# Causal masking of the diagonal blocks moved from two-pass score matmuls to Pool, in a one-core pre-norm transformer layer

## The chip, the cores and the metric

The kernel runs on one core of one Trainium2 chip. The metric is the device time of one launch in microseconds. A core has a matrix engine (PE: matmuls, with weight loads shown apart as PEld), a vector engine (DVE), a scalar engine (ACT), a general engine (Pool) and SyncE (SP), whose queue issues the DMAs here. Each runs its own instructions in order and they meet by semaphores.

## The reference

One attention block with ALiBi bias and causal mask, then a gated feed-forward block with ternary weights, both with a layer norm ahead and a residual. T = 2048 tokens, D = 256, 16 heads of 16, hidden 704.

```
s = q @ k.T / 4 + slope[h] * (key - 2047)          # per head; the bias hangs on the key alone
s = where(key <= query, s, lowest float)
attn = softmax(s);  x = x + (attn @ v) @ Wo + bo
x = x + bitlinear(sigmoid(bitlinear(n, w1)) * bitlinear(n, w2), w3)    # n = layernorm(x)
```

## The kernel before

Queries are taken in four chunks of 512 (c = 0 to 3), heads in four groups of four; chunk times group makes 16 units. A unit of chunk c walks over 4(c+1) key blocks of 128: that is a **step**, 160 in all. In one step each of the four heads gets one transposed score tile, keys on the partitions and up to 512 queries along the row. The last four steps of a unit are its **diagonal steps** (64 in all; in chunk 0 every step is one): there the tile starts at the diagonal block (`q0`), so its width is 512, 384, 256 and 128.

A score matmul (L928) contracts two stacks of 128 rows, `kst` and `qst`: 64 rows of query and key in split high and low parts, two rows of ALiBi, padding, and two rows that subtract the row maximum. On a diagonal step a second matmul (L931, bf16, an identity times the 128x128 triangle `maskb`) adds -3e38 to the future keys of the diagonal block. ACT then takes exp from PSUM into a slot of `probs` (L775; seven slots, three PSUM banks), and PE multiplies the slot with the values (L941, `weighted`; ones beside the values give the denominators).

PE's order is written out: in step s come scores of head 0, head 1, a **side group** (projections, feed-forward matmuls of a neighbouring chunk), head 2, then `weighted(s-1)` for the four heads, then head 3. After each head's scores stand **max turns** of the next unit (L908: scores the other way round, into three banks `pM`), which DVE reduces to row maxima (L1078, L1081 with mask). The turns are dealt out over the steps by a planned room of DVE. A unit's maxima then go to `qst` by DMA (L448) before its first score.

Pool's work per step is one instruction group in order: `split_lo` (L671, gates the store of q and k parts, and ACT's next projection), `split_hidden` (L650, L652, gates the down projection), setting up of stack rows (`key_rows` L658 and `query_rows` L663, L664), `add_bo` (L641), `norm_ctx` (L603) and `power` for the layer norm (L632, DVE's `normalise` L999 waits for it). The head of the program builds `ident`, `mask`, `maskb` on Pool (L613 to L625), then loads the first stacks through SP (`load_k` L427, L429; `load_q` L442), whose landing the first turn waits for.

Of the kernel before, what the change touches and what calls it, by code (L numbers as in the profile page):

```python
# [16 lines left out]
def preln_layer(nc, x, Wq, bq, Wk, bk, Wv, bv, Wo, bo, w1, w2, w3, alibi, out):  # L17
# [24 lines left out]
    R_END = P  # L42
    R_MAX = R_END - 2
    KSLOTS, QSLOTS, PSLOTS = 7, 4, 7
# [9 lines left out]
    phase0 = [first_step[c * NHG] for c in range(NCH)] + [NS]  # L54
    steps = [(u, j) for u in range(NU) for j in range(n_steps[u])]


# [39 lines left out]

    POST_AT = [None, 10, 22, 41]
    late = [("up", NCH - 2, 1, FT - 2), ("up", NCH - 2, 1, FT - 1), ("down", NCH - 2, 1)]
# [101 lines left out]
    with es:  # L201
# [42 lines left out]
        ones = flat[:, 6 * CH:6 * CH + P]  # L244
        w_abs = flat[:, 0:FT * D]
        x2T = sb("x2T", [P, 2, KT, HALF], F32R)
        hT = sb("hT", [P, 2, FT, HALF], F32R)
        mask = sb("mask", [P, CH], BF16)
        maskb = sb("maskb", [P, P], BF16)
        ident = sb("ident", [P, P])  # L250
# [51 lines left out]
        const_ok = sem("const_ok")  # L302
        pad_ok = sem("pad_ok")
        rows_ok = sem("rows_ok")
        k_rows = sem("k_rows")
# [23 lines left out]
        scores_ready = sem("scores_ready")  # L329
        probs_ready = sem("probs_ready")  # L330
        pv_done = sem("pv_done")
        ctx_saved = sem("ctx_saved")
# [13 lines left out]
        def diag(u, j):  # L346

            return max(0, j - TPC * units[u][0]) * P

        def is_diag(u, j):  # L350
            return j >= TPC * units[u][0]

# [25 lines left out]
        def _(sp):  # L378
# [37 lines left out]
            def load_k(n):  # L416
                v, i = pieces[n]
                parts_there("k", i, units[v][1])
                if n >= KSLOTS:

                    pu, pi = pieces[n - KSLOTS]
                    sp.wait_ge(scores_ready, G * (first_step[pu] + TPC * pi + TPC))
                if n < KSLOTS:
                    sp.wait_ge(k_rows, n + 1)
                hg = units[v][1]
                src = part_rows(1, i, hg).rearrange("d (p a) h n -> (d p) a (h n)", a=1)
                sp.dma_start(kst[0:R_ALIBI, n % KSLOTS, :, :].bitcast(F32),  # L427
                             src.to_broadcast([2 * HD, 2, G * CH])).then_inc(k_in[n % KSLOTS], 16)
                sp.dma_start(kst[R_ALIBI:R_ALIBI + 2, n % KSLOTS, :, :].bitcast(F32),  # L429
                             alibi_parts[:, hg * G:(hg + 1) * G, i * CH:(i + 1) * CH])\  # L430
                    .then_inc(k_in[n % KSLOTS], 16)

            def load_q(v):
# [6 lines left out]
                for a in range(2):  # L440
                    src = part_rows(0, c, hg)[:, a:a + 1, :, :].rearrange("d a h n -> d a (h n)")
                    sp.dma_start(qst[a:R_ALIBI:2, v % QSLOTS, :, :].bitcast(F32),  # L442
                                 src.to_broadcast([HD, 2, G * CH])).then_inc(q_in[v % QSLOTS], 16)

            def load_m(v):
# [144 lines left out]
        def _(pool):  # L590
# [18 lines left out]
            for i in range(2):  # L609
# [10 lines left out]
                                         fill=NEG, base=0, pattern=[[-1, P]], channel_multiplier=1))  # L620
            link(nc.gpsimd.memset(maskb[:, :], 0.0))

            link(nc.gpsimd.affine_select(out=maskb[:, :], in_=maskb[:, :], compare_op=ALU.is_ge, fill=NEG,
                                         base=0, pattern=[[1, P]], channel_multiplier=-1))
            nc.gpsimd.memset(ones, 1.0).then_inc(const_ok, 1)  # L625

            pool.wait_ge(const_ok, 1)


# [31 lines left out]
            def query_rows(n):  # L661
# [3 lines left out]
                pool.wait_ge(q_rows, n + 1)  # L665

            def split_lo(g):
                i = split_no[g]
# [6 lines left out]
            power(1)  # L675
            query_rows(0)
            split_lo(("k", 0, 0))
            power(2)
# [10 lines left out]
            for s, (u, j) in enumerate(steps):  # L689
                c = units[u][0]  # L690
                ph = s - phase0[c]
                g = side[s]
                if g and g[0] in "kq":
                    split_lo(g)
# [4 lines left out]
                if ph == 2 and c >= 1:  # L699
                    add_bo(c - 1)  # L700
                if c >= 1 and ph == POST_AT[c] - 2:
                    norm_ctx(c - 1)
# [113 lines left out]
        def _(pe):  # L816
# [80 lines left out]
            def max_turn(u, k):  # L897
                i, h, t = turn_of(u, k)
                c = units[u][0]
                if k == 0:  # L900
                    pe.wait_ge(q_in[u % QSLOTS], Q_DMAS * 16 * (u // QSLOTS + 1))
                n = piece0[u] + i
                if h == 0 and t == 0:
                    pe.wait_ge(k_in[n % KSLOTS], K_DMAS * 16 * (n // KSLOTS + 1))
                x = ("turn", u, k)
# [12 lines left out]
            def scores(s, h):  # L918
# [4 lines left out]
                if j == 0 and h == 0:  # L923
# [3 lines left out]
                b = j % TPC * P  # L927
                ins = pe.matmul(pS[:, n % SBANKS, q0:CH], kst[0:R_END, sl, h, b:b + P],  # L928
                                qst[0:R_END, u % QSLOTS, h, q0:CH], start=True, stop=not is_diag(u, j))
                if is_diag(u, j):  # L930
                    ins = pe.matmul(pS[:, n % SBANKS, q0:q0 + P], identb[:, :], maskb[:, :], start=False, stop=True)  # L931
                ins.then_inc(scores_ready, 1)

            def weighted(s):
# [4 lines left out]
                for h in range(G):  # L939
                    pe.wait_ge(probs_ready, G * s + h + 1)  # L940
                    pe.matmul(pO[32 * h:32 * h + VW, q0:CH], vals[:, j, units[u][1] * G + h, :],  # L941
# [282 lines left out]
```

## Time and profile before

| | us |
|---|---|
| median of 3 runs | 697.68 (695.25 to 704.3) |
| profiled execution | 701.53, its span 698.6 |
| granted TensorE clock, mean | 0.972 |

The span is the time between the first and the last instruction; the execution's time is 2.9 us more. Busy shares of PE are of modelled ends; matmuls are pipelined, so distances between starts tell what a matmul costs.

### The profile page before, as it was taken

Reading aid. Unit: us, or ns where it says so; the run is one execution under the profiler, and the core shown is the slowest. Engines: PE = TensorE matmul, PEld = TensorE weight load, DVE = VectorE, ACT = ScalarE, POOL = GpSimd, SP = SyncE. Lnnn points to the kernel's source line nnn. Section 1 sums busy time; section 2 is a strip of 40 time slices with the busy share of each in tenths; the row PEclk is TensorE's granted clock in tenths of the full one; section 3 lists DMA queues with packets and bytes.
Section 4 is the critical chain, followed back from the end, with each engine's and each line's share of the span. In section 5 each row is a group of like instructions: output and inputs, shape, how many; then the busy total and the mean of one; then the engine's idle time right before and its main releaser. Section 6 shows DMA issues by size and latency. Waiting matters only on the chain.

```text
span 698.6 us, 10974 instructions
## 1 busy us (share of the span) xinstructions
PE 644.3 (92%) x3710; PEld 373.3 (53%) x3710; DVE 469.8 (67%) x1189; ACT 373.5 (53%) x770; POOL 119.8 (17%) x148
## 2 busy tenths in 40 slices
PE   1788898999999989999999999999999999899997
PEld 1444554546465555455555565555454555456486
DVE  4377858767876866668787778778778787511076
ACT  2424454664564435656655545466576675486621
POOL 5485000041021111320001212003100000031200
PEclk9969988999999999999999999999999999999999
DMA  8665564465131312543221131136131120011000
GB/s 247 179 161 152 138 142 108 95 198 140 32 77 33 92 32 69 177 124 79 62 72 39 32 91 33 47 90 164 44 76 33 47 64 0 2 41 40 1 16 30
DMA packets 26635, 57.64 MB, mean 83 GB/s; under 512 B 4756, under 2 KB 14484, under 8 KB 22996
## 3 DMA queue, kind: packets, MB, share of 16 engines
q1 hardware_dynamic: 26580, 56.95, 31.5%
q8 instruction: 29, 0.48, 0.3%
q14 instruction: 26, 0.21, 0.1%
HBM read 41.87 MB, written 14.80 MB: 81 GB/s over the span
## 4 chain that ended last, share of the span: by engine, by line
PE 79%; DVE 11%; issue 3%; DMA 3%; ACT 2%; SPq 1%; POOL 1%; POOLq 0%; DVEq 0%; ACTq 0%
PE pS L928 20%; PE pO L941 19%; PE pM L908 18%; PE pW L883 5%; DVE pm L1078 3%; PE pW L829 3%; PE pW L892 3%; DVE pM L1081 2%; PE pS L931 2%; PE pW L869 2%; PE pW L835 2%; PE pS L892 1%; DMA qst<-mT 1%; PE pS L829 1%; PE pS L883 1%
## 5 line engine op out<-in xcount | busy, mean ns | idle before, releaser
L775 ACT ACTIVATE probs<-pS 128x512 f32<-128x512 f32 (+3 forms) x640 | 312.9, 536 | 259.9 <-PE pS L931 127.8
L1078 DVE TENSOR_REDUCE pm<-pM 128x1 f32<-128x512 f32 x384 | 243.9, 683 | 70.5 <-PE pM L908 69.8
L908 PE MATMUL pM<-kst,qst 126*128 126x512 f32 (+3 forms) x640 | 244.0, 408 | 17.6 <-DVE pm L1081 7.7
L928 PE MATMUL pS<-qst,kst 128*128 128x512 f32 (+3 forms) x640 | 255.4, 416 | 4.0 <-DMA qst<-mT 3.3
L928 PEld LDWEIGHTS pS<-qst,kst 128*128 128x128 f32 x640 | 121.7, 193 | 138.2 <-ACT probs L775 112.1
L1081 DVE CUSTOM_DVE_ANT_0 pM<-pM,mask 128x128 f32<-128x128 f32 (+3 forms) x256 | 120.7, 514 | 72.0 <-PE pM L908 71.1
L941 PE MATMUL pO<-probs,vals 128*17 128x512 f32 (+3 forms) x1280 | 151.1, 543 | 0.0
L908 PEld LDWEIGHTS pM<-kst,qst 126*128 126x128 f32 x640 | 124.4, 199 | 49.7 <-DVE pm L1081 16.9
L931 PE MATMUL pS<-maskb,identb 128*128 128x128 bf16 x256 | 59.5, 234 | 0.0
L632 POOL TENSOR_TENSOR rstd<-ve,mhalf 128x4 f32<-128x4 f32 (+1 forms) x9 | 8.5, 945 | 240.5 <-DVE ve L994 240.4
L941 PEld LDWEIGHTS pO<-probs,vals 128*17 128x17 f32 x1280 | 21.4, 95 | 42.4 <-issue 31.8
L931 PEld LDWEIGHTS pS<-maskb,identb 128*128 128x128 bf16 x256 | 25.1, 98 | 31.0 <-issue 23.3
L650 POOL CAST hT<-work 128x256 fp32r<-128x256 f32 (+1 forms) x34 | 13.5, 396 | 160.1 <-DVE work L1046 135.3
L1081 DVE DVE_READ_ACCUMULATOR2_ANT pm<- 128x1 f32 x256 | 36.2, 141 | 0.0
L671 POOL TENSOR_TENSOR qk_hl<-qk_f,qk_hl 128x512 fp32r<-128x512 f32 x16 | 20.4, 1275 | 78.4 <-ACT qk_hl L732 78.2
L1046 DVE SCALAR_TENSOR_TENSOR work<-work,pW 128x256 f32<-128x256 f32 (+1 forms) x38 | 15.7, 414 | 26.6 <-ACT work L765 24.1
L883 PE MATMUL pW<-x2T,w1T 128*128 128x256 f32 (+1 forms) x144 | 24.9, 295 | 4.1 <-DVE x2T L1039 2.4
L652 POOL TENSOR_TENSOR hT<-work,hT 128x256 fp32r<-128x256 f32 (+1 forms) x34 | 25.0, 735 | 2.7
L883 PEld LDWEIGHTS pW<-x2T,w1T 128*128 128x128 f32 (+1 forms) x144 | 19.9, 182 | 8.7 <-DVE x2T L1039 2.8
L883 PE MATMUL pW<-x2T,w2T 128*128 128x256 f32 (+1 forms) x144 | 23.4, 285 | 0.0
L883 PEld LDWEIGHTS pW<-x2T,w2T 128*128 128x128 f32 (+1 forms) x144 | 19.8, 184 | 0.0
L892 PE MATMUL pW<-w3T,hT 128*128 128x256 f32 (+1 forms) x120 | 18.1, 295 | 0.3 <-DVE x2T L1039 0.3
(145 smaller groups left out, 425.1 us busy)
## 6 DMA issues: line engine op xcount, KB each, us to landing
kst<-parts SPq DMA_DIRECT2D x40, 512.0 KB
parts<-qk_hl SPq DMA_DIRECT2D x32, 256.0 KB, 3.0
qst<-parts SPq DMA_DIRECT2D x32, 256.0 KB, 4.3
ctx_dram<-ctx_raw SPq DMA_DIRECT2D x15, 256.0 KB, 4.7
xin<-in_L_attn_x SPq DMA_DIRECT2D x5, 512.0 KB, 5.4
out<-work SPq DMA_DIRECT2D x8, 256.0 KB, 2.2
work<-ctx_dram SPq DMA_DIRECT2D x7, 256.0 KB
work<-rden_dram SPq DMA_DIRECT2D x7, 256.0 KB
```

The source lines that it names most:

```text
L652: nc.gpsimd.tensor_tensor(hT_of(g)[0:rows, 1, m, :], hid[0:rows, i % 2, :], hT_of(g)[0:rows, 0, m, :].bitcast(F32), ALU.subtract).then_inc ...
L671: nc.gpsimd.tensor_tensor(lo.bitcast(F32R), qk_f[:, :], hi, ALU.subtract).then_inc(split_ok, 1)
L775: nc.scalar.activation(probs[:, n % PSLOTS, q0:CH], pS[:, n % SBANKS, q0:CH], ACT.Exp)\
L829: ins = pe.matmul(w, (wk_s if kind == "k" else wq_s)[:, k, g[2] * P:(g[2] + 1) * P], xnT[:, k, :], start=k == 0, stop=k == KT - 1)
L883: ins = pe.matmul(w[0:r, i * HALF:(i + 1) * HALF], wT[:, k, m * P:m * P + r], x2T_of(g)[:, part, k, :], start=k == 0 and part == 0, stop=k ...
L892: ins = pe.matmul(w[:, i * D:(i + 1) * D], hT_of(g)[0:r, part, f, i * P:(i + 1) * P], w3T[0:r, f, :], start=f == 0 and part == 0, stop=f = ...
L908: pe.matmul(max_bank(x)[:, 0:N], qst[0:R_MAX, u % QSLOTS, h, t * P:(t + 1) * P], kst[0:R_MAX, n % KSLOTS, h, 0:N], start=True, stop=True). ...
L928: ins = pe.matmul(pS[:, n % SBANKS, q0:CH], kst[0:R_END, sl, h, b:b + P], qst[0:R_END, u % QSLOTS, h, q0:CH], start=True, stop=not is_diag ...
L931: ins = pe.matmul(pS[:, n % SBANKS, q0:q0 + P], identb[:, :], maskb[:, :], start=False, stop=True)
L941: pe.matmul(pO[32 * h:32 * h + VW, q0:CH], vals[:, j, units[u][1] * G + h, :], probs[:, (G * s + h) % PSLOTS, q0:CH], start=j == 0, stop=j ...
L1078: nc.vector.tensor_reduce(dst, bank, AX.X, ALU.max).then_inc(max_free, 1)
L1081: nc.vector.tensor_tensor_reduce(out=sc, in0=sc, in1=mask[:, CH - (t + 1) * P:CH], scale=1.0, scalar=NEG, op0=ALU.add, op1=ALU.max, accum_ ...
```

## The change

The future keys of the diagonal block are no longer pushed down in PSUM. ACT takes exp of the raw tile, and Pool then sets the future keys of the 128x128 diagonal block in the slot to zero with one select (`clear_future`), 256 in all, ahead of its other work of the step; PE's `weighted` waits for Pool (`causal_ok`) on diagonal steps. The 256 matmuls of L931 and `maskb` are gone. Four rows of each stack (124 to 127) are given to half blocks: row b is 1 for the upper half of the keys of block b, and -2^100 for the lower half of the queries of block b, so that the quadrant furthest in the future is exp(-huge) = 0. The two rows of the maximum move to 122 and 123; off the diagonal the matmul uses 124 rows. Pool builds these rows once (`cut_rows`), SP copies them into the 7 + 4 stack slots (`load_cut`), and the slots' semaphores count 16 more. `norm_ctx` in chunk 2 comes one step earlier (at step 19 of the chunk in place of 20; 8 and 39 stay in chunks 1 and 3).

```diff
+    R_CUT = R_END - TPC
+    R_MAX = R_CUT - 2
+    FAR = -2.0 ** 100
-    POST_AT = [None, 10, 22, 41]
+    POST_AT, NORM_AT = [None, 10, 22, 41], [None, 8, 19, 39]
@@ SP
             def load_k(n):
...
+                if n < KSLOTS:
+                    load_cut(kst, cut_k, n, k_in, K_DMAS)
+            def load_cut(stack, cut, n, landed, dmas):
+                if n == 0:
+                    sp.wait_ge(cut_ok, 1)
+                    src = cut
+                else:
+                    sp.wait_ge(landed[0], (dmas + 1) * 16)
+                    src = stack[R_CUT:R_END, 0, 0, :].bitcast(F32)
+                sp.dma_start(stack[R_CUT:R_END, n, :, :].bitcast(F32),
+                             src.rearrange("p (a n) -> p a n", a=1).to_broadcast([TPC, G, CH]))\
+                    .then_inc(landed[n], 16)
@@ Pool
-            link(nc.gpsimd.memset(maskb[:, :], 0.0))
-            link(nc.gpsimd.affine_select(out=maskb[:, :], in_=maskb[:, :], ...))
+            def cut_rows():
+                link(nc.gpsimd.memset(cut_k, 0.0))
+                link(nc.gpsimd.memset(cut_q, 0.0))
...
+                link(nc.gpsimd.affine_select(out=upper, in_=upper, compare_op=ALU.not_equal, fill=1.0, ...))
+                nc.gpsimd.affine_select(out=lower, in_=lower, ..., fill=FAR, ...).then_inc(cut_ok, 1)
+            def clear_future(s, h):
+                u, j = steps[s]
+                n, q0 = G * s + h, diag(u, j)
+                pool.wait_ge(probs_ready, n + 1)
+                block = probs[:, n % PSLOTS, q0:q0 + P]
+                nc.gpsimd.affine_select(out=block, in_=block, compare_op=ALU.is_ge, fill=0.0, base=0,
+                                        pattern=[[1, P]], channel_multiplier=-1).then_inc(causal_ok, 1)
...
             query_rows(0)
+            cut_rows()
             split_lo(("k", 0, 0))
...
+                if on_diag[s]:
+                    for h in range(G):
+                        clear_future(s, h)
+                    pool.wait_ge(causal_ok, G * diag_before[s + 1])
                 if g and g[0] in "kq":
                     split_lo(g)
...
-                if c >= 1 and ph == POST_AT[c] - 2:
+                if ph == NORM_AT[c]:
                     norm_ctx(c - 1)
@@ PE
-                ins = pe.matmul(pS[:, n % SBANKS, q0:CH], kst[0:R_END, sl, h, b:b + P],
-                                qst[0:R_END, u % QSLOTS, h, q0:CH], start=True, stop=not is_diag(u, j))
-                if is_diag(u, j):
-                    ins = pe.matmul(pS[:, n % SBANKS, q0:q0 + P], identb[:, :], maskb[:, :], start=False, stop=True)
-                ins.then_inc(scores_ready, 1)
+                rows = R_END if on_diag[s] else R_CUT
+                pe.matmul(pS[:, n % SBANKS, q0:CH], kst[0:rows, sl, h, b:b + P], qst[0:rows, u % QSLOTS, h, q0:CH], start=True, stop=True).then_inc(scores_ready, 1)
             def weighted(s):
...
-                    pe.wait_ge(probs_ready, G * s + h + 1)
+                    if on_diag[s]:
+                        pe.wait_ge(causal_ok, G * diag_before[s] + h + 1)
+                    else:
+                        pe.wait_ge(probs_ready, G * s + h + 1)
```

## Rows read from the trace of the kernel before

**Rows 1.** The page: busy us (share of the span) and instructions, part 1
```profile
PE 644.3 (92%) x3710; PEld 373.3 (53%) x3710; DVE 469.8 (67%) x1189; ACT 373.5 (53%) x770; POOL 119.8 (17%) x148
```
**Rows 2.** The page: lines of the chain that ended last, part 4
```profile
PE pS L928 20%; PE pO L941 19%; PE pM L908 18%; PE pW L883 5%; DVE pm L1078 3%; PE pW L829 3%; PE pW L892 3%; DVE pM L1081 2%; PE pS L931 2%; PE pW L869 2%; PE pW L835 2%; PE pS L892 1%; DMA qst<-mT 1%; PE pS L829 1%; PE pS L883 1%
```
**Rows 3.** Windows: chunk 0, chunk 1 with the start of 2; stretch, busy (instructions), clock, DMA
```profile
49.90:128.50 78.60, 67.77 (x395) 38.78 (x394) 57.43 (x182) 36.03 (x80) 11.45 (x8) 0.89 0.52 126
128.50:333.00 204.50, 196.78 (x1126) 113.82 (x1127) 144.41 (x363) 112.41 (x233) 36.86 (x46) 0.99 0.38 98
```
**Rows 4.** The same view, a unit's four diagonal steps in chunk 3 (columns PE, PEld, DVE, ACT, POOL)
```profile
497.20:508.60 11.40, 11.40 (x80) 5.66 (x79) 8.96 (x23) 6.81 (x16) 0.00 (x0) 1.00 0.21 50
```
**Rows 5.** Timeline of PE, off the diagonal: scores and turns, 512 wide (start, duration)
```profile
514.17 0.40 PE L928 MATMUL pS<-qst,kst 128*128 128x512 f32 x1
514.40 0.40 PE L908 MATMUL pM<-kst,qst 126*128 126x512 f32 x1
514.64 0.39 PE L928 MATMUL pS<-qst,kst 128*128 128x512 f32 x1
```
**Rows 6.** Timeline of PE, on the diagonal: scores 384 wide, mask matmul, turn
```profile
501.42 0.33 PE L928 MATMUL pS<-qst,kst 128*128 128x384 f32 x1
501.60 0.23 PE L931 MATMUL pS<-maskb,identb 128*128 128x128 bf16 x1
501.64 0.48 PE L908 MATMUL pM<-kst,qst 126*128 126x512 f32 x1
501.95 0.33 PE L928 MATMUL pS<-qst,kst 128*128 128x384 f32 x1
```
**Rows 7.** Timeline, start of Pool's work: select, next instruction; memset 512 wide
```profile
2.11 0.29 POOL L614 TENSOR_SCALAR_AFFINE_SELECT ident<-ident 128x128 f32<-128x128 f32 x1 [0.24 <-POOL ident L613]
2.46 0.29 POOL L616 CAST identb<-ident 128x128 bf16<-128x128 f32 x1
2.81 0.53 POOL L617 MEMSET mask<- 128x512 bf16 x1
```
**Rows 8.** Timeline: ACT ends, Pool starts; Pool ends, ACT starts
```profile
21.15 0.68 ACT L732 ACTIVATE qk_hl<-pS,bias_k 128x512 fp32r<-128x512 f32 x1
21.98 1.26 POOL L671 TENSOR_TENSOR qk_hl<-qk_f,qk_hl 128x512 fp32r<-128x512 f32 x1 [9.64 <-ACT qk_hl L732]
23.33 0.69 ACT L731 ACTIVATE qk_f<-pS,bias_q 128x512 f32<-128x512 f32 x1 [1.50 <-POOL qk_hl L671]
```
**Rows 9.** Timeline, a unit's third diagonal step: exps (head 3 first), weighted matmuls
```profile
506.80 0.55 ACT L775 ACTIVATE probs<-pS 128x256 f32<-128x256 f32 x2 [1.06 <-PE pS L931]
507.86 0.63 PE L941 MATMUL pO<-probs,vals 128*17 128x256 f32 x8
```
**Rows 10.** Timeline of Pool and PE at the end of chunk 1
```profile
264.14 1.01 POOL L632 TENSOR_TENSOR rstd<-ve,mhalf 128x4 f32<-128x4 f32 x1
265.16 0.84 PE L941 MATMUL pO<-probs,vals 128*17 128x384 f32 x8
```
**Rows 11.** Timeline of SP and PE in the head: first loads, first turn
```profile
27.89 0.49 SPq L429 DMA_DIRECT2D kst<-alibi_parts  x1
29.70 1.19 SPq L442 DMA_DIRECT2D qst<-parts  x2
35.07 1.12 PE L908 MATMUL pM<-kst,qst 126*128 126x128 f32 x3 [3.31 <-DMA qst<-parts]
```
**Rows 12.** Timeline of DVE: normalise beside Pool's memset, and alone
```profile
8.63 4.50 DVE L999 TENSOR_SCALAR xin<-xin,mv,rstd 128x256 f32<-128x256 f32 x4 [1.22 <-POOL rstd L632]
125.84 1.36 DVE L999 TENSOR_SCALAR xin<-xin,mv,rstd 128x256 f32<-128x256 f32 x4
```
**Rows 13.** Timeline: Pool's long work beside a reduction of DVE
```profile
490.10 2.67 POOL L603 TENSOR_TENSOR work<-work 128x512 f32<-128x512 f32 x2 [6.95 <-DMA work<-rden_dram]
490.78 0.69 DVE L1078 TENSOR_REDUCE pm<-pM 128x1 f32<-128x512 f32 x1 [0.58 <-PE pM L908]
```
**Rows 14.** Timeline of ACT: the last exp of the last step
```profile
661.26 0.28 ACT L775 ACTIVATE probs<-pS 128x128 f32<-128x128 f32 x1 [0.61 <-PE pS L931]
```

More of the change, by code:

```diff
@@ L42, in preln_layer @@
     R_END = P
-    R_MAX = R_END - 2
+    R_CUT = R_END - TPC
+    R_MAX = R_CUT - 2
+    FAR = -2.0 ** 100
     KSLOTS, QSLOTS, PSLOTS = 7, 4, 7
@@ L55, in preln_layer @@
     steps = [(u, j) for u in range(NU) for j in range(n_steps[u])]
+    on_diag = [j >= TPC * units[u][0] for u, j in steps]
+    diag_before = [sum(on_diag[:s]) for s in range(NS + 1)]
     piece0 = [sum(units[v][0] + 1 for v in range(u)) for u in range(NU + 1)]
@@ L245, in preln_layer @@
         w_abs = flat[:, 0:FT * D]
+        cut_k, cut_q = ctx_raw[0:TPC, :], probs[0:TPC, 3, :]
         x2T = sb("x2T", [P, 2, KT, HALF], F32R)
@@ L248, in preln_layer @@
         mask = sb("mask", [P, CH], BF16)
-        maskb = sb("maskb", [P, P], BF16)
         ident = sb("ident", [P, P])
@@ L303, in preln_layer @@
         pad_ok = sem("pad_ok")
+        cut_ok = sem("cut_ok")
         rows_ok = sem("rows_ok")
@@ L330, in preln_layer @@
         probs_ready = sem("probs_ready")
+        causal_ok = sem("causal_ok")
         pv_done = sem("pv_done")
@@ L348, in diag @@
             return max(0, j - TPC * units[u][0]) * P
-        def is_diag(u, j):
-            return j >= TPC * units[u][0]
         def max_bank(x):
@@ L443, in load_q @@
                                  src.to_broadcast([HD, 2, G * CH])).then_inc(q_in[v % QSLOTS], 16)
+                if v < QSLOTS:
+                    load_cut(qst, cut_q, v, q_in, Q_DMAS)
             def load_m(v):
@@ L620, in _ @@
                                          fill=NEG, base=0, pattern=[[-1, P]], channel_multiplier=1))
-            link(nc.gpsimd.memset(maskb[:, :], 0.0))
-            link(nc.gpsimd.affine_select(out=maskb[:, :], in_=maskb[:, :], compare_op=ALU.is_ge, fill=NEG,
-                                         base=0, pattern=[[1, P]], channel_multiplier=-1))
             nc.gpsimd.memset(ones, 1.0).then_inc(const_ok, 1)
             pool.wait_ge(const_ok, 1)
+            def cut_rows():
+                link(nc.gpsimd.memset(cut_k, 0.0))
+                link(nc.gpsimd.memset(cut_q, 0.0))
+                upper = cut_k.rearrange("p (b e n) -> p b e n", b=TPC, e=2)[:, :, 1, :]
+                lower = cut_q.rearrange("p (b e n) -> p b e n", b=TPC, e=2)[:, :, 0, :]
+                link(nc.gpsimd.affine_select(out=upper, in_=upper, compare_op=ALU.not_equal, fill=1.0, base=0,
+                                             pattern=[[-1, TPC], [0, P // 2]], channel_multiplier=1))
+                nc.gpsimd.affine_select(out=lower, in_=lower, compare_op=ALU.not_equal, fill=FAR, base=0,
+                                        pattern=[[-1, TPC], [0, P // 2]], channel_multiplier=1).then_inc(cut_ok, 1)
+                pool.wait_ge(cut_ok, 1)
             def power(n, t0=0, t1=TPC):
@@ L900, in max_turn @@
                 if k == 0:
-                    pe.wait_ge(q_in[u % QSLOTS], Q_DMAS * 16 * (u // QSLOTS + 1))
+                    pe.wait_ge(q_in[u % QSLOTS], 16 + Q_DMAS * 16 * (u // QSLOTS + 1))
                 n = piece0[u] + i
                 if h == 0 and t == 0:
-                    pe.wait_ge(k_in[n % KSLOTS], K_DMAS * 16 * (n // KSLOTS + 1))
+                    pe.wait_ge(k_in[n % KSLOTS], 16 + K_DMAS * 16 * (n // KSLOTS + 1))
                 x = ("turn", u, k)
```

## The prediction, made before the changed kernel was run

> **What bounds the kernel now.** I read the page's busy shares first, then the lines of the chain, then the windows of each chunk, and at last the timelines of single steps. PE is busy 92% of the span, DVE 67%, Pool 17% [rows 1]. The chain runs over PE's scores, weighted matmuls and max turns for 57% of the span, and DVE's reductions for 5% [rows 2]. By chunk: in chunk 0 PE is busy 67.8 of 78.6 us and DVE 57.4, at a granted clock of 0.89, so both take turns to hold up the other; from chunk 1 into chunk 2 PE is busy 196.8 of 204.5 us and DVE 144.4, 71% [rows 3]. In the four diagonal steps of a unit of chunk 3 PE has no idle time at all in 11.40 us, and DVE has 8.96 us of work [rows 4]. So PE's order of matmuls sets the time, and DVE stands 21% behind it just where the change works.
>
> **The mask matmul's price.** Its busy time of 0.23 us [rows 6] is no price, since matmuls overlap. Distances between starts are: off the diagonal a score tile and a turn, both 512 wide, repeat every 0.47 us (514.17 to 514.64), of which the score tile takes 0.23 and the turn 0.24 [rows 5]. On the diagonal a 384-wide score tile, the mask and a turn repeat every 0.53 us [rows 6]. Without the mask the tile would take 384/512 of 0.23, that is 0.17, and the turn 0.24: 0.41. The mask costs 0.12 us. In the start times only 0.04 of that stands between the mask and the turn (501.60 to 501.64); the rest is that the turn's successor starts 0.31 after it, in place of 0.24. Lower bound: 0.04, the mask's own distance. Upper bound: the whole 0.23 of its busy time, as if nothing overlapped. I take 0.12, because it compares whole repeats.
>
> A rule of the Trainium skill differs: "TensorE: Matmul & The Clock Gate", section Back-to-back issue gap, puts a stream of weight load and matmul pairs at N = 128 at about 81 ns each. By that estimate 256 of them are 20.7 us, of which the shares taken below leave 15.8, 11.9 net: 686 us. The trace's repeats give 0.12 a piece, half as much again.
>
> In chunks 1 to 3 there are 48 diagonal steps with 192 masks: 192 x 0.12 = 23.0 us of PE. A unit's four diagonal steps lose 16 x 0.12 = 1.9 us, 11.40 to 9.5, with DVE's 8.96 unchanged: DVE goes to 94%. It may run only three banks apart from PE, so some of PE's gain turns into waits for turns; I take 85%, 19.6 us. The bound for this is DVE's own 8.96: no more than 2.4 us a unit, 29 us for 12 units. In chunk 0, 64 x 0.12 = 7.7 us, and since DVE holds PE for part of it I take half, 3.8 us. Gain: 23.4 us.
>
> **What Pool adds.** 256 selects of 128x128 f32. The same form took 0.29 us, and the next instruction started 0.35 us after it [rows 7]. Four a step are 1.4 us, 90 us in all; Pool goes from 17% to some 30%. That is under the mean diagonal step of chunk 3, 11.40 / 4 = 2.85 now and 2.4 after [rows 4]. DVE's reductions read PSUM and take no harm: one took 0.69 us in the middle of a Pool instruction of 2.67 [rows 13].
>
> What counts is the delay from the last exp of a step (head 3) to `weighted`. ACT's end to Pool's start took 0.15 (21.83 to 21.98), Pool's end to the next engine 0.09 (23.24 to 23.33) [rows 8]: 0.15 + 0.29 + 0.09 = 0.53 us. PE leaves room for it, since `weighted(s-1)` stands behind three score tiles of the next step. The room is tightest in a unit's third diagonal step, whose tiles are narrow while the next ones are narrower still: two exps take 0.55 us from 506.80, so head 3's ends near 507.15, and the weighted matmuls start at 507.86: 0.7 us [rows 9]. The mask of the score tile in between goes out of that room, 0.12, and a little more as PE comes sooner: some 0.5 is left, level with the 0.53. I take 0.1 us of stall in each of 12 units, 1.2 us; the wider steps have more room. Queued behind that wait on PE are head 3's scores and the next step; ACT waits for these.
>
> **The in-order queue of Pool.** In a diagonal step the clears stand ahead of `split_lo`, `split_hidden` and `power`, which then wait for the last exp of the step. These ran a step later than PE's start of it anyway, because DVE or ACT were later. The other way round, a clear waits behind the previous step's work. This bites once: at the end of chunk 1 `power` ends at 265.15 and the weighted matmuls of the next diagonal step started at 265.16 [rows 10]; four clears after it are 4 x 0.35 = 1.4 us, of which I take 1.2 on the path. The other long Pool works (`add_bo`, `norm_ctx`) have steps off the diagonal between them and the next clear; uncovered they would cost their own 1.3 us each. Moving `norm_ctx` costs nothing for that reason. `key_rows` of slots 4 to 6 slide some microseconds later in chunk 0, ahead of loads seven steps on.
>
> **Head and tail.** `cut_rows` adds two memsets and two selects 512 wide; a 512-wide memset took 0.53 [rows 7], so some 2.5 us, less 0.6 for `maskb`. Pool was idle for 9.64 us before its first split [rows 8]: hidden; uncovered it is 1.9 us. SP issues 11 small DMAs of some 0.49 us each, the price of the alibi rows' issue [rows 11]. The one for keys falls in the gap from 28.38 to 29.70. The one for queries is issued behind the two of L442 that end at 30.89, whose landing releases the first turn at 35.07 [rows 11]. It lands 0 to 1 us after them; I take 0.5 us. The nine later ones wait only for slot 0's landing, long past. The rows are taken from padding, and 124 or 128 rows make the same columns, so I put that at nothing. At the end, the last exp ended at 661.54 and ACT's copy of the context waits for the weighted matmuls behind it [rows 14]: there the 0.53 less the direct hand-off of 0.1 is bare, 0.4 us. The last unit has no turns, so its room is smaller: 3 steps x 0.2 = 0.6.
>
> **The two-port rule.** DVE's `normalise` took 4.50 us beside a Pool memset and 1.36 alone [rows 12]. Three of them fall in diagonal steps. If each meets Pool's 1.4 us of clears, 3 x 1.4 = 4 us at most; DVE is not the bound there and I count nothing, but keep 4 for the range. This is what the Trainium skill says in "GPSIMD Engine Reference", section 1, Specifications: Pool shares its SBUF interfaces with DVE instructions in a two-port mode. The trace agrees; by the rule at its full price the forecast would be 682 us.
>
> **Sum.** Gain 23.4; costs 1.2 + 1.2 + 0.5 + 0.4 + 0.6 = 3.9; net 19.5. The profiled execution took 701.5 us (span 698.6 and 2.9 around it), 3.8 above the median of 697.7. 701.5 - 19.5 = 682.0 in its own time, and 697.7 - 19.5 = 678.2, so 678 us, against the median.
>
> **Rivals.**
>
> *PE's gain turns into waits for DVE, or the mask was cheaper than a repeat shows.* For it: 94% for DVE after the change, three banks, and the 0.04 between mask and turn; 2% of the span is L931's share of the chain, 14 us [rows 2]. Against it: whole repeats. If half the 23.4 stays, 11.7 - 3.9 = 8 us net, 690 us; with the chain's 14 us, 10 net, 688. Time: 689 us.
>
> *Pool becomes the bound of the diagonal steps (slower).* Place: the four clears of each of the 48 diagonal steps of chunks 1 to 3, on Pool one behind another, with `weighted` waiting for the last. After the change such a step has 2.4 us of PE (9.5 / 4). With t from one select's start to the next, Pool needs 4t: it fills the step at t = 0.6; it eats the net 19.5 us at 4t = 2.4 + 19.5 / 48, t = 0.70; it makes the kernel slower by 2% at 48 x (4t - 2.4) = 19.5 + 14, t = 0.77. At t = 0.85: 48 x 1.0 = 48 us, 697.7 - 19.5 + 48 = 726 us. For it: Pool's spans are rough, the one row of this form is of the idle head, and Pool's 512-wide work takes 1.26 us [rows 8]. Against it: the row gives t = 0.35 [rows 7], less than half of what is needed.
>
> *The mask was dearer.* At 0.18 a mask and DVE in step, 29 us in chunks 1 to 3 and 6 in chunk 0, less 4: 31 net, 667 us.
>
> **How the numbers follow.** Chances: forecast 0.55 (its own range 671 to 683), DVE or cheap mask 0.27, Pool late 0.10, dearer mask 0.08. Faster by over 2%, which is about what a measurement of this kernel can tell from no change (below 683.7): 0.55 + 0.08 = 0.63. Within 2%: 0.27. Slower: 0.10. The range goes from 668 (the dearer mask) to 692 (the lower bound of 0.04 a mask still gives 256 x 0.04 = 10, less the costs of 4, that is 691.5).
>
> **What the changed profile would show.** No L931; score tiles 384 wide and turns repeating every 0.41 to 0.43 us; a unit's four diagonal steps in chunk 3 at 9.5 to 10 us in place of 11.40, with DVE busy over 90% of them; Pool at about 30% with selects of 0.29 us; PE's waits for Pool at `weighted` under 5 us in all. I would be wrong if the four diagonal steps stay above 10.7 us, if selects take over 0.5 us, or if waits for max turns grow by over 8 us.

## The result and the profile after

The changed kernel takes 690.71 us (median of 4 runs, 686.79 to 692.86) beside 697.68 before: a ratio of 0.988, 95% interval 0.983 to 0.993. By that ratio it is faster by 1.2%, and by the two medians by 7.0 us, where 19.5 us (2.8%) were forecast. The time lies inside the forecast's outer range (668 to 692) and outside the forecast's own (671 to 683). Single executions of one kernel lie up to 9 us apart, and the profiled one of the changed kernel, 686.79 with a span of 684.9, was the fastest of its four, so its span of 13.7 us less overstates the gain. Steps inside the profiles repeat far better, and the accounts below are made in them.

One thing has to be kept apart there: the clock that TensorE was granted, which has two levels, 1.2 and 2.4 GHz (0.5 and 1.00 in the profile). Unit 14's steps off the diagonal took 44.36 us at a mean of 0.97 in the kernel before, and 42.97 at 1.00 in the changed kernel: those 1.4 us are no effect of the change, for kernel e2 below, which has the change as well, took 44.15 at 0.97. In the kernel before it fell to 0.50 at 597.8 us, after PE had been busy for 6.20 of 7.80 us; what made it fall was not found. Where two kernels are compared below at unequal clock, the text says so.

The page of the changed kernel, part 1, and three of its groups (line, engine, operation, count, busy us, mean ns, idle before and releaser):

```profile
PE 619.7 (90%) x3454; PEld 360.1 (53%) x3454; DVE 473.1 (69%) x1189; ACT 367.4 (54%) x770; POOL 197.4 (29%) x406
...
L981 PE MATMUL pO<-probs,vals 128*17 128x512 f32 (+3 forms) x1280 | 152.1, 540 | 1.2 <-POOL probs L699 1.2
L699 POOL TENSOR_SCALAR_AFFINE_SELECT probs<-probs 128x128 f32<-128x128 f32 x256 | 74.8, 305 | 245.2 <-ACT probs L815 240.0
L981 PEld LDWEIGHTS pO<-probs,vals 128*17 128x17 f32 x1280 | 22.1, 95 | 46.4 <-issue 35.4 <-POOL probs L699 6.0 <-ACT probs L815 2.2
```

256 matmuls are gone, and Pool stands at 29%, as forecast; a select takes 0.305 us on average in the dense phase, so the price of [rows 7] held. PE's weight loads waited for Pool at the weighted matmuls for 6.0 us in all; what that cost is measured in e2.

The same windows view as [rows 4], the four diagonal steps of unit 12 in the changed kernel:

```profile
487.50:498.00 10.50, 10.40 (x64) 5.24 (x63) 8.85 (x23) 6.21 (x16) 4.21 (x15) 1.00 0.22 53
```

11.40 us became 10.50 with DVE's work unchanged; 9.5 was forecast. PE's timeline in the second of these steps answers to [rows 6]:

```profile
491.02 0.34 PE L969 MATMUL pS<-qst,kst 128*128 128x384 f32 x1
491.20 0.40 PE L948 MATMUL pM<-kst,qst 122*128 122x512 f32 x1
491.43 0.34 PE L969 MATMUL pS<-qst,kst 128*128 128x384 f32 x1
491.61 0.40 PE L948 MATMUL pM<-kst,qst 122*128 122x512 f32 x1
```

The repeat is 0.41 us where it was 0.53: just what was forecast. So the measured repeat was right, and yet half of the time expected from it is missing in this unit. PE's weight loads in the same stretch show some of it, waits that were not there before (in brackets: idle before, releaser):

```profile
488.43 0.19 PEld L948 LDWEIGHTS pM<-kst,qst 122*128 122x128 f32 x1 [0.22 <-DVE pm L1121]
...
489.08 0.19 PEld L948 LDWEIGHTS pM<-kst,qst 122*128 122x128 f32 x1 [0.35 <-DVE pm L1121]
...
492.03 0.19 PEld L948 LDWEIGHTS pM<-kst,qst 122*128 122x128 f32 x1 [0.22 <-DVE pm L1121]
...
496.74 0.19 PEld L969 LDWEIGHTS pS<-qst,kst 128*128 128x128 f32 x1 [0.33 <-ACT probs L815]
```

Three turns wait for a bank that DVE holds, and in the fourth, narrowest step a score tile waits for ACT to release one of the three score banks. Over the whole kernel the idle time before the turns' weight loads grew from 49.7 to 67.5 us (pages of before and after):

```profile
L908 PEld LDWEIGHTS pM<-kst,qst 126*128 126x128 f32 x640 | 124.4, 199 | 49.7 <-DVE pm L1081 16.9
```
```profile
L948 PEld LDWEIGHTS pM<-kst,qst 122*128 122x128 f32 x640 | 122.7, 193 | 67.5 <-DVE pm L1121 25.7
```

The prediction named growth of over 8 us in the waits for turns as a sign of being wrong. Of the idle time before these loads DVE ended 30.5 us before and 40.1 after, 9.6 more; before the turns' matmuls themselves the idle time grew less, from 17.6 to 23.8. In the 48 diagonal steps of chunks 1 to 3 alone, the turns' loads waited for DVE for 7.0 us and then for 13.4, and the idle time before the score tiles' loads went from 36.5 to 40.7.

Three theories were put to the test. **P**: Pool's clears and the longer head took the missing gain back. **W**: PE's freed time turned into waits for DVE and ACT. **C**: the mask matmul was cheaper than priced.

### The profile page after: what moved, and what is told of

Same layout as the page of the kernel before. It is cut to its first block, busy times and chain, and to the rows that moved or that the text cites. A ratio compares the mean times of both kernels' runs of the same rounds, so it can differ in the third digit from the quotient of the medians.

```text
span 684.9 us, 10797 instructions
## 1 busy us (share of the span) xinstructions
PE 619.7 (90%) x3454; PEld 360.1 (53%) x3454; DVE 473.1 (69%) x1189; ACT 367.4 (54%) x770; POOL 197.4 (29%) x406
## 4 chain that ended last, share of the span: by engine, by line
PE 77%; DVE 13%; issue 4%; DMA 2%; ACT 2%; POOL 1%; SPq 0%; POOLq 0%; DVEq 0%; ACTq 0%
PE pS L969 20%; PE pO L981 19%; PE pM L948 17%; PE pW L923 6%; DVE pm L1118 3%; PE pW L869 3%; DVE pM L1121 3%; PE pW L932 3%; PE pW L909 2%; PE pW L875 2%; PE pS L932 1%; PE pS L869 1%; PE pS L923 1%; ACT probs L815 1%; DVE st L1027 1%
## 5 line engine op out<-in xcount | busy, mean ns | idle before, releaser
L815 ACT ACTIVATE probs<-pS 128x512 f32<-128x512 f32 (+3 forms) x640 | 307.1, 536 | 249.7 <-PE pS L969 246.0
L948 PE MATMUL pM<-kst,qst 122*128 122x512 f32 (+3 forms) x640 | 231.7, 390 | 23.8 <-DVE pm L1121 9.6
L969 PE MATMUL pS<-qst,kst 124*128 124x512 f32 (+4 forms) x640 | 249.2, 410 | 3.6 <-DMA qst<-mT 1.7
L969 PEld LDWEIGHTS pS<-qst,kst 124*128 124x128 f32 (+1 forms) x640 | 118.1, 190 | 141.6 <-ACT probs L815 113.5
L948 PEld LDWEIGHTS pM<-kst,qst 122*128 122x128 f32 x640 | 122.7, 193 | 67.5 <-DVE pm L1121 25.7
L699 POOL TENSOR_SCALAR_AFFINE_SELECT probs<-probs 128x128 f32<-128x128 f32 x256 | 74.8, 305 | 245.2 <-ACT probs L815 240.0
L677 POOL CAST hT<-work 128x256 fp32r<-128x256 f32 (+1 forms) x34 | 13.5, 396 | 92.7 <-DVE work L1086 79.9
L706 POOL TENSOR_TENSOR qk_hl<-qk_f,qk_hl 128x512 fp32r<-128x512 f32 x16 | 21.8, 1364 | 43.5 <-ACT qk_hl L772 43.0
L865 PE MATMUL pW<-ident,xin 128*128 128x128 f32 x24 | 4.1, 300 | 15.5 <-DVE xin L1039 15.1
```

The costliest lines, as they stand in the source:

```text
L699: nc.gpsimd.affine_select(out=block, in_=block, compare_op=ALU.is_ge, fill=0.0, base=0, pattern=[[1, P]], channel_multiplier=-1).then_inc( ...
L706: nc.gpsimd.tensor_tensor(lo.bitcast(F32R), qk_f[:, :], hi, ALU.subtract).then_inc(split_ok, 1)
L815: nc.scalar.activation(probs[:, n % PSLOTS, q0:CH], pS[:, n % SBANKS, q0:CH], ACT.Exp)\
L948: pe.matmul(max_bank(x)[:, 0:N], qst[0:R_MAX, u % QSLOTS, h, t * P:(t + 1) * P], kst[0:R_MAX, n % KSLOTS, h, 0:N], start=True, stop=True). ...
L969: pe.matmul(pS[:, n % SBANKS, q0:CH], kst[0:rows, sl, h, b:b + P], qst[0:rows, u % QSLOTS, h, q0:CH], start=True, stop=True).then_inc(scor ...
```

## The experiments

Step times are distances between first score tiles of steps, from PE's timeline. "Diagonal, chunks 1 to 3" is the sum over the 48 diagonal steps. Medians of before lay between 696.6 and 699.0 us in the three sittings. Unit 7's diagonal steps ran at a granted clock of 0.91 or 0.92 in before, e1, e2, e3, e4 and e8, and at 1.00 in the others; e8 is the changed kernel with two instructions of its head in another order, so in these steps it is the changed kernel at the clock of before.

| kernel | median us | unit 12, four diagonal steps | diagonal, chunks 1 to 3 | first score tile |
|---|---|---|---|---|
| before | 697.7 | 11.39 (3.66 3.04 2.63 2.05) | 179.5 | 49.96 |
| changed | 690.7 | 10.45 (3.47 2.74 2.35 1.90) | 168.0 | 51.62 |
| e1 before, masks gone | 687.4 | 10.45 (3.46 2.74 2.35 1.90) | 168.3 | 49.16 |
| e2 changed, no clears | 688.6 | 10.43 (3.47 2.73 2.35 1.89) | 168.6 | 52.02 |
| e3 before, light turns | 679.6 | 11.22 (3.49 3.06 2.63 2.05) | 173.9 | 48.05 |
| e4 changed, light turns | 666.9 | 10.00 (3.13 2.62 2.35 1.89) | 162.5 | 50.95 |
| e6 before, weighted late | 683.4 | 11.19 (3.65 3.07 2.56 1.91) | 169.4 | 51.90 |
| e5 changed, weighted late | 670.6 | 10.03 (3.40 2.64 2.25 1.74) | 158.6 | 51.61 |
| e9 before, late and light | 667.3 | 11.02 (3.48 3.06 2.56 1.92) | 166.3 | 48.10 |
| e7 changed, late and light | 654.1 | 9.77 (3.15 2.63 2.25 1.74) | 153.9 | 51.14 |
| e8 changed, head reordered | 691.0 | 10.44 (3.46 2.73 2.36 1.89) | 169.4 | 51.66 |

**e1: the removal alone.**

```
-                qst[..., q0:CH], start=True, stop=not is_diag(u, j))
-                if is_diag(u, j):
-                    ins = pe.matmul(pS[..., q0:q0 + P], identb[:, :], maskb[:, :], start=False, stop=True)
+                qst[..., q0:CH], start=True, stop=True)
-                nc.scalar.activation(probs[...], pS[...], ACT.Exp)
+                nc.scalar.activation(probs[...], pS[...], ACT.Exp, scale=0.01)
```

> The kernel before without its 256 mask matmuls and with nothing in their place: the future keys of the diagonal blocks are not masked, and exp takes 0.01 of the score so that it stays finite. It measures the removal alone. If Pool's clears and the longer head took the missing gain back (theory P), this kernel shows the forecast gross gain of 20 us or more, some 675 us beside 697.7 of before, and four diagonal steps of a unit of chunk 3 near 9.5 us. If PE's freed time turns into waits for DVE and ACT (theory W), the gain is 9 to 13 us, 685 to 689, those four steps stay near 10.4 us, and the score and turn repeats still shorten from 0.53 to 0.41. If the mask was simply cheap (theory C), the gain is the same 9 to 13 but the repeats stay near 0.47.

Measured: 687.4 us beside 699.0 (0.985, 0.979 to 0.991), and unit 12's four steps at 10.45, to 0.01 us those of the changed kernel, with no clear anywhere. The removal itself brings 11.6 us and not over 20. Theory P falls for the diagonal steps. Of the two others, the expectation gave W the repeats of 0.41 us and C repeats of 0.47. In the second step of unit 12 they are 0.41, twice: this run speaks for W, and against C in the form that was written down.

**e2: the changed kernel without the clears.** `clear_future` is not called, and `weighted` waits for `probs_ready`.

> The changed kernel without Pool's 256 clears; the weighted matmuls wait for exp as before. Left out: the future keys of the diagonal blocks count in the softmax (except the far quadrant). Theory P: 8 to 12 us faster than the changed kernel, 679 to 683, and the four diagonal steps of unit 12 go from 10.45 to under 9.8 us. Theory W: at most 3 us faster, those four steps at 10.2 to 10.4 us, since the trace shows PE waiting for Pool at weighted for 6 us in all, most of it level with other waits.

Measured: 688.6 us (0.986, 0.982 to 0.990; the changed kernel's 0.988 had 0.983 to 0.993) and 10.43 in unit 12. The 256 selects, 75 us of Pool, cost nothing in the median that can be told from zero. In the diagonal steps of chunks 1 to 3 at the same clock, 168.6 us stand here beside e8's 169.4: 0.8 us for the selects, 0.5 of it in unit 7 and 0.3 in unit 5.

**e3 and e4: DVE's turns cut in half, in both kernels.** The first pair that tells W from C.

```
-                    nc.vector.tensor_reduce(dst, bank, AX.X, ALU.max)
+                    nc.vector.tensor_reduce(dst, bank[:, 0:CH // 2], AX.X, ALU.max)
-                    sc = bank[:, 0:(t + 1) * P]
+                    sc = bank[:, 0:(t + 1) * P // 2]
```

> The kernel before with DVE's reductions of the max turns cut to half their columns (the maxima are then wrong; exp takes 0.01 of the score to stay finite). PE, ACT and Pool do all their work. It is the base of the next run. Both theories: chunk 0 gets faster, the four diagonal steps of unit 12 stay at 11.2 to 11.4 us because PE has no idle time in them; 680 to 690 us.

> The changed kernel with the same half reductions. Theory W with DVE as the waiting partner: the four diagonal steps of unit 12 fall from 10.45 to 9.6 to 9.8 us, and this kernel beats the run before it by 14 us or more, where the full kernels differ by 7 to 8. Theory P or C: these steps stay at 10.3 or more, and the difference stays 7 to 9 us.

Windows of unit 12's four diagonal steps, e3 and then e4 (PE, PEld, DVE, ACT, Pool busy):

```profile
478.70:489.90 11.20, 11.20 (x79) 5.57 (x79) 6.27 (x23) 6.81 (x16) 0.00 (x0) 1.00 0.22 51
```
```profile
468.60:478.60 10.00, 9.93 (x63) 5.26 (x63) 5.90 (x23) 6.17 (x16) 4.21 (x15) 1.00 0.23 56
```

DVE's work went from 8.96 to 6.27 and 5.90 us. The difference of the two kernels in unit 12 grew from 0.94 to 1.22: lighter turns gave back 0.28 us a unit, not the 1 us that was missing. Over all 48 diagonal steps the difference is 11.4 us (173.9 less 162.5). Beside the 11.5 of the full kernels (179.5 less 168.0) that is no growth, but there the changed kernel had the better clock in unit 7; with e8 in its place the full kernels differ by 10.1, and the growth is 1.3 us. The expectation of 9.6 to 9.8 for W was missed at 10.00, and so was that of 10.3 or more for C. The medians lie 12.7 us apart, between the two expectations. W's part with DVE holds in part. Halves of the reductions do not take DVE's waits away: the page of e4 still has 45.1 us of idle time before the turns' weight loads, that of e3 32.9.

**e5 and e6: the weighted matmuls behind head 3, in both kernels.**

```
-                    if h == 2 and s:
+                    if h == 3 and s:
                         weighted(s - 1)
```

> The changed kernel with the weighted matmuls of step s-1 moved behind the score tile of head 3 (they stood behind that of head 2). ACT's exp of head 3 then runs while PE does the weighted matmuls, so the score tile of head 2 of the next step no longer waits for it. If the three score banks hold PE in the narrow steps (theory W, part ACT), the four diagonal steps of unit 12 fall from 10.45 to 9.9 to 10.1 us and the kernel gains 3 to 6 us, 685 to 688. If what is left is DVE alone, they stay at 10.3 or more and the time stays within 2 us of the changed kernel.

> The same move in the kernel before. PE has no idle time in the diagonal steps there, so both theories: the four steps of unit 12 stay at 11.2 to 11.4 us, time within 3 us of before. If it gains as much as in the changed kernel, the score banks had nothing to do with the missing gain.

In the changed kernel the four steps came to 10.03, as W expected, and the kernel to 670.6 us (0.960, 0.954 to 0.966), far more than the 3 to 6 us expected. In the kernel before they stayed at 11.19, as expected, but the kernel gained 13.5 us all the same, where 3 at most were expected (683.4; 0.979, 0.972 to 0.986). Their difference over the diagonal steps of chunks 1 to 3 is 10.8 us, and in unit 12 it grew from 0.94 to 1.16: the order of the weighted matmuls is a gain of its own, and adds little to what the masks are worth there. In the kernel before it lies in chunks 1 to 3: 10.1 us in the diagonal steps and 7.0 beside them, less 2.6 in the head and chunk 0 of that execution, whose chunk 0 had a clock of 0.87 beside 0.89. ACT's side work stands between the exps of heads 2 and 3, so that the exp of head 3, which PE waits for, was the late one in steps with a side group; that this is the mechanism is argued, not shown.

**e7 and e9: both edits in both kernels.** Meant to give the mask's price with the waits out of the way.

> The changed kernel with both: half reductions in the max turns and the late weighted matmuls. If DVE and the score banks together hold all of the missing time, the four diagonal steps of unit 12 come to the forecast 9.5 us; the halves alone gave 10.0. If they stay at 9.9 or more, the distance between starts priced the mask too high for the narrow steps.

> The kernel before with the late weighted matmuls and half reductions: the base for the run of the changed kernel with both (654.1 us, the four diagonal steps of unit 12 at 9.77). With waits for DVE and for ACT out of the way in both, the difference of these four steps, over 16, is the mask matmul's price on PE. If the distance between starts priced it well, they stand at 11.2 us or more here, 1.4 to 1.5 of difference, 0.09 a mask or more, and the whole kernel is 16 to 20 us behind 654.1. If the mask is worth 0.06, they stand at 10.8.

Windows of unit 12 in e9 and e7:

```profile
467.50:478.50 11.00, 11.00 (x82) 5.64 (x78) 5.94 (x21) 6.66 (x16) 0.00 (x0) 1.00 0.21 52
```
```profile
460.00:469.80 9.80, 9.80 (x67) 5.11 (x63) 5.67 (x21) 6.27 (x16) 4.24 (x15) 1.00 0.22 57
```

PE shows no idle time in either, DVE under 60% work. The difference, 11.02 less 9.77, is 1.25 us for 16 masks: 0.078 a mask, between the 0.09 and the 0.06 that were named. By step it is 0.33, 0.43, 0.31 and 0.18 us for four masks each. But the waits are not out of the way in e7. PE's weight loads there show three in unit 12 that e9 does not have; two of them, in the first and the fourth step:

```profile
461.33 0.19 PEld L948 LDWEIGHTS pM<-kst,qst 122*128 122x128 f32 x1 [0.21 <-DVE pm L1121]
...
468.62 0.19 PEld L969 LDWEIGHTS pS<-qst,kst 128*128 128x128 f32 x1 [0.18 <-ACT probs L815]
```

The third is 0.09 us for DVE, in the third step. Over the 48 diagonal steps the idle time before the score tiles' loads is 30.7 us in e9 and 36.8 in e7, that before the turns' loads which DVE ended 2.4 and 5.1. The fourth step shows what such a wait does. In e9 two score tiles stand one behind the other, with their masks:

```profile
477.15 0.22 PE L928 MATMUL pS<-qst,kst 128*128 128x128 f32 x1
477.21 0.23 PE L931 MATMUL pS<-maskb,identb 128*128 128x128 bf16 x1
477.25 0.31 PE L928 MATMUL pS<-qst,kst 128*128 128x128 f32 x1
477.40 0.23 PE L931 MATMUL pS<-maskb,identb 128*128 128x128 bf16 x1
477.44 0.48 PE L908 MATMUL pM<-kst,qst 126*128 126x512 f32 x1
```

The way from the first tile to the turn is 0.29 us, and in e7, without the masks, 0.30: the second tile waits for its bank, and what two masks had cost goes into that wait. So 0.078 is a lower bound of the price in unit 12; with the three waits added in full (0.21 + 0.18 + 0.09) it would be 0.108. Over all diagonal steps of chunks 1 to 3 this pair differs by 12.3 us, 0.064 a mask, a lower bound too. The medians lie 13.2 apart.

**The price by place.** The order of PE's instructions is the same in both kernels but for the masks, so the distance from each score tile to the next can be compared one by one. Sorted by what PE does next behind the mask, for the 191 masks of chunks 1 to 3 that have a score tile behind them, before less changed:

| behind the mask | masks | distance shorter by, median us |
|---|---|---|
| a turn, tile of 256 to 512 columns | 102 | 0.12 |
| a turn, tile of 128 columns | 26 | 0.077 |
| another score tile | 40 | 0.043 |
| weighted matmuls | 9 | 0.073 |
| a side group | 14 | 0.065 |

e1, e2 and e8 give the same medians within 0.01. So the mask has no single price: it is 0.12 us before a turn, as forecast, and about a third of that before another score tile. Taken at these medians the masks add up to 17.4 us, 0.091 each. The measured sum is 11.5, and 10.1 at equal clock (e8); the 6 to 7 us between are places where the distance shrank by less or grew. In unit 12 there are five such places among 16, and at four of them stand the waits shown above (488.43, 489.08, 492.03, 496.74). The medians price that unit's masks at 1.53 us, and 0.94 were gained. That the remainder is waits is shown for these four places; for the other units it rests on the idle times before the weight loads, which grew by 10.6 us in the same steps (the score tiles', and the turns' that DVE ended). So W and C both hold: of the 23.0 us at which the prediction priced these masks, 5.6 were never there (C) and 6 to 7 went into waits (W).

**e8: Pool's first memset moved behind `power`.** The changed kernel's first score tile is 1.66 us late. Its timeline at the start, all engines (start, duration, engine, line, operation; in brackets the idle time before and its releaser), down to the first turn:

```profile
4.16 1.80 POOL L685 MEMSET kst<- 64x2048 f32 x1
4.78 1.32 DVE L1149 CAST probs<-probs 128x256 fp32r<-128x256 f32 x1 [4.78 <-DMA probs<-alibi]
...
9.84 5.08 DVE L1039 TENSOR_SCALAR xin<-xin,mv,rstd 128x256 f32<-128x256 f32 x4 [1.22 <-POOL rstd L659]
...
15.06 1.09 PE L865 MATMUL pW<-ident,xin 128*128 128x128 f32 x4 [15.06 <-DVE xin L1039]
...
31.87 0.70 SPq L446 DMA_DIRECT2D qst<-probs  x1
...
36.96 3.80 PE L948 MATMUL pM<-kst,qst 122*128 122x128 f32 x9 [4.25 <-DMA qst<-probs]
```

> The changed kernel with Pool's first key_rows memset moved behind the power instruction. In the changed kernel this memset starts at 4.16 us, before DVE's first copy (4.78), which then takes 1.32 us in place of 0.29; before, two instructions for the triangle mask held the memset back to 4.80. If that overlap made the head late, DVE's copy is back at 0.29 us and the first score tile starts near 50.5 us in place of 51.62. If the late head is the new DMAs alone, it stays at 51.4 or more. The whole time moves by 1 us, which only the profile can show.

The same stretch of e8's timeline:

```profile
4.69 0.29 DVE L1149 CAST probs<-probs 128x256 fp32r<-128x256 f32 x1 [4.69 <-DMA probs<-alibi]
...
8.72 5.75 DVE L1039 TENSOR_SCALAR xin<-xin,mv,rstd 128x256 f32<-128x256 f32 x3 [1.22 <-POOL rstd L659]
8.74 1.80 POOL L685 MEMSET kst<- 64x2048 f32 x1
...
15.23 1.09 PE L865 MATMUL pW<-ident,xin 128*128 128x128 f32 x4 [15.23 <-DVE xin L1039]
```

The copy is back at 0.29 us, as expected, but the memsets now all fall on `normalise` (three of the four in this window; the four take 6.36 us), and the first score tile stays at 51.66, where 50.5 was expected. The overlap had moved, not gone. The median is 691.0 us, the changed kernel's within the noise.

**e10: the head mended** (on e5): Pool waits for the end of DVE's first `normalise` before the memsets, and the two copies into slot 0 are issued before the first stores of parts.

```
-            key_rows(0)
             power(1)
+            pool.wait_ge(xn_ok, 1)
+            key_rows(0)
...
+            load_cut(kst, cut_k, 0, k_in, K_DMAS)
+            load_cut(qst, cut_q, 0, q_in, Q_DMAS)
             sp.wait_ge(al_out, 32)
```

> The changed kernel with the late weighted matmuls (670.6 us), and two edits in the head: Pool's memsets of the first stack rows wait until DVE's first normalise is done, and the two copies of half-block rows into slot 0 are issued before the first stores of parts, where SP waits anyhow. If the late head is Pool's memsets against DVE (some 3 us in normalise) and the copy queued behind the query loads (0.9 us), the first turn starts near 33 us in place of 36.96, the first score tile near 48 us in place of 51.6, and the kernel gains 3 to 4 us. If DVE's slow normalise was not on the path, the first turn stays at 35 or later.

The timeline of e10 at its start (Pool, DVE, PE):

```profile
8.92 1.38 DVE L1042 TENSOR_SCALAR xin<-xin,mv,rstd 128x256 f32<-128x256 f32 x4 [1.22 <-POOL rstd L661]
10.42 1.80 POOL L687 MEMSET kst<- 64x2048 f32 x1 [1.54 <-DVE xin L1042]
...
13.89 1.09 PE L868 MATMUL pW<-ident,xin 128*128 128x128 f32 x4 [13.89 <-ACT wq_s L829]
...
34.99 2.25 PE L951 MATMUL pM<-kst,qst 122*128 122x128 f32 x6 [3.46 <-DMA qst<-parts]
```

`normalise` takes 1.38 us, PE starts at 13.89 in place of 15.06 and now waits for ACT's copy of a weight, as the kernel before did (14.12), which is a likely reason why the 33 and 48 us expected were not reached. The first turn starts at 34.99, where the kernel before had 35.07, the first score tile at 49.97. Both edits of the head were made at once, so their shares were not measured apart. The median is 667.7 us (0.959, 0.955 to 0.963), within the noise of e5; the 1.6 us show in the profile alone.

**e11: a new plan for the turns** (on e5): `room` of the diagonal steps times 0.85.

> The changed kernel with the late weighted matmuls, and the planner's room of the diagonal steps cut to 0.85, since these steps are now shorter on PE: turns move to the other steps. If the turns are dealt for the old step lengths, the four diagonal steps of unit 12 fall from 10.03 to about 9.8 us and the other steps stay near 3.07 us: 2 to 4 us gained. If DVE is evenly loaded, what is won on the diagonal is lost beside it, within 2 us.

Unit 12's four steps fell to 9.87 in place of the 9.8 expected, and its other twelve rose from 36.86 to 37.58: won on the diagonal, lost beside it. 669.2 us, within the noise of e5.

**e12: all three edits.**

> All three edits on the changed kernel: late weighted matmuls, the head, the plan. If they add up: 670.6 less 3.5 and less 2, some 665 us, 4.5% below the kernel before.

667.4 us (0.957, 0.954 to 0.960): the same as e10 and short of the 665 expected, 4.3% below the kernel before. The plan adds nothing.

## Why the prediction was wrong

*PE's order bounds the kernel.* Right: taking 256 matmuls away from PE moved the time, and e1 equals the changed kernel to 0.01 us in the steps of unit 12.

*The mask's price, 0.12 us, and the 85% of it that PE was to keep.* **This is the step that failed**, in both its factors. The repeat of [rows 6] was read rightly and did go to 0.41. But it is the price before a turn, and it was taken for all 192. By place, 102 of the 191 compared are worth 0.12, and the others 0.04 to 0.08: 17.4 us in place of 23.0. And waits took 6 to 7 us of that, over a third, where 15% (3.4 us) was allowed: the change brought 11.5 us in the diagonal steps of chunks 1 to 3, 10.1 at equal clock, where 19.6 were forecast. In unit 12: forecast 1.9 us before the waits; 1.53 by place; 0.94 measured. The mechanism that was named for the 85%, PE running three banks apart from DVE, is real and was too small, and a second one was left out: PE waits for ACT at the three score banks as well. How the waits divide between the two is not settled, since each of the two edits gave back some of the same time: the difference in unit 12 is 0.94 us as it is, 1.22 with light turns, 1.16 with the weighted matmuls late, 1.25 with both. Why a mask costs less before a score tile than before a turn is open.

The estimate by the Trainium skill was the nearer one here: the 81 ns of "TensorE: Matmul & The Clock Gate", section Back-to-back issue gap, stand beside the 91 of the price by place, and its 686 us beside 690.7. The single places, 43 to 120 ns, do not keep to that one figure.

*Chunk 0, 3.8 us.* 78.6 us before; 75.8 in the changed kernel's profile, but at a granted clock of 0.93 beside 0.89. At 0.89 it is 76.6 in e1 and 76.5 in e8: 2.0 to 2.1 us, about half of the forecast. Between other pairs it differs by up to 7.4 us (e6 and e5, 0.87 and 0.93), so a single pair of profiles settles little there.

*Pool's clears, 0.53 us of delay and 1.2 + 0.6 us of stalls.* The hand-off was priced well and the stalls are less: 10.43 us without clears, 10.45 with them in unit 12, and 0.1 us in the last unit (8.58 and 8.69). In the third diagonal step of unit 12 head 3's clear is the last thing that the weighted matmuls wait for, and they start 0.6 us behind the exp, level with PE's own arrival.

*Pool's queue at the end of chunk 1, 1.2 us.* The wait came: PE stood idle for 0.88 us before the weighted matmuls at 260.13, released by Pool. Unit 7's diagonal steps took 20.54 us with clears (e8) and 20.01 without (e2) at the same clock, so it cost some 0.5 us. The 19.09 of the changed kernel's own profile are at a clock of 1.00 and do not compare.

*The head, 0.5 us.* It cost 1.66 at the first score tile, and 1.89 at the first turn (36.96 for 35.07), in two parts. The copy of the query rows behind the query loads held the first turn for some 0.95 us: its issue takes 0.70 and not the 0.49 of the alibi rows. The other 0.94 is PE's later start (15.06 for 14.12) and came from what was *removed*: without the two `maskb` instructions Pool's memset began at 4.16 instead of 4.80 and met DVE's copy. I had priced these two instructions at nothing, on Pool's own idle time, and weighed the two-port effect [rows 12] for the diagonal steps alone, where it did not show.

*The tail, 0.4 us.* 0.3 (38.09 from the last score tile to the end, 37.81 before). *124 or 128 rows, nothing:* right, twelve steps of unit 12 off the diagonal took 36.63 and 36.62 us.

*The rivals.* "PE's gain turns into waits, or the mask was cheaper" was given 0.27 and 689 us; that is what happened, both halves of it at once. It was put too low because the arguments for it, DVE's 94% and L931's 2% of the chain, 14 us, were outweighed by one clean repeat. The rival's halved gain of 11.7 us and the chain's 14 were nearer to the 11.6 of e1 than the forecast's 23.4; the halving was a guess and not a measurement.

Steps and medians agree as far as they can. e8's profile, which has the clock of before in chunk 0 and unit 7, is 10.0 us shorter than that of before (688.6 for 698.6). The profiled execution of before was 3.8 us over its median, which leaves 6.2 us beside the 7.0 of the medians.

## What to carry to other kernels

Price an instruction between two others over all the places where it stands, sorted by its neighbours, and not in the cleanest repeat. Then ask at each place what else PE would have to wait for there: here over a third of the price went into waits for two other engines. An experiment that is to take waits away must show that they are gone, in the weight loads' idle time and not in PE's busy time alone. Compare stretches at the same granted clock. When a kernel removes work from an idle engine, ask what now starts earlier and whom it meets. And look at what an engine waits for last before taking work from it: here one line of order on PE was worth 13.5 us in the old kernel, as much as all the mask matmuls (11.6 in e1; the intervals overlap).

## What the runs showed of the hardware that was not expected

A DVE copy of 128x256 f32 in SBUF took 1.32 us in place of 0.29 when it met a Pool memset, and four `normalise` instructions took 5.08 us, and 6.36 in e8, in place of 1.38. The slow instructions end when the memset does: the copy at 6.10 us, 0.15 behind the end of the memset that began at 4.16, and all four `normalise` of the changed kernel's head 0.14 to 0.15 us behind the end of a memset, whether it was one of 1.80 us (2048 columns) or of 0.55 (512 columns). So each was held for as long as the memset ran. Not every DVE instruction is: in the kernel before, a `tensor_tensor` and four `bn_stats` ran beside such a memset (4.80 to 6.63) in 0.43 and 1.41 us, and without one they took 0.43 and 1.40 in e8.

```profile
4.80 1.83 POOL L658 MEMSET kst<- 64x2048 f32 x1
4.93 0.43 DVE L1110 TENSOR_TENSOR probs<-probs 128x256 fp32r<-128x256 f32 x1
...
5.39 1.41 DVE L987 BATCH_NORM_STATS2 st<-xin 128x6 f32<-128x256 f32 x4
```

Beside Pool's selects in the diagonal steps no such hold appeared: four `normalise` took 1.45 us (259.74 to 261.19) while clears ran beside them. DVE's and Pool's rows of the changed kernel's timeline there:

```profile
259.74 1.45 DVE L1039 TENSOR_SCALAR xin<-xin,mv,rstd 128x256 f32<-128x256 f32 x4 [0.96 <-POOL rstd L659]
...
259.78 2.08 POOL L699 TENSOR_SCALAR_AFFINE_SELECT probs<-probs 128x128 f32<-128x128 f32 x7
```

Seven selects back to back take 2.08 us there, 0.30 each. A select is shorter than one `normalise` (0.40), so a hold until its end would hardly show; whether the selects do not hold DVE or only hold it too briefly was not tried.
